# Register loads of TensorE in two separated steps, and the last tiles' upward products in two halves around the downward ones

## What is computed

```python
x = x + tanh(g_xattn) * xattn(layernorm(x), ctx, itok, Wq, Wkv, Wo)   # 16 heads, each query looks at 4 neighbouring keys
h = layernorm(x)
gate_probs = softmax(h @ gate_w.T)          # 8 experts
top_v, top_i = top_k(gate_probs, 2)         # each token goes to two of them
for e in range(8):
    y = silu(h @ w1[e] + b1[e]) @ w2[e] + b2[e]     # 256 -> 1024 -> 256
    out += y * comb_w[..., e]
x = x + tanh(g_ffn) * out
```

## Time and profile before

| | us |
|---|---|
| median of 3 runs | 349.89 |
| lowest and highest | 349.18 and 349.98 |
| the profiled execution | 349.19 |
| its span in the profile | 347.5 |
| TensorE busy | 316.7 |
| VectorE busy | 259.5 |
| POOL busy | 198.0 |
| ScalarE busy | 174.2 |

### The profile page before, as it was taken

The page is one execution under the profiler, slowest core; times in us unless marked ns, Lnnn a source line. Parts: engine busy times, 40 slices in busy tenths (PEclk is TensorE's granted clock), DMA queues, the critical chain, the costliest instruction groups (busy, mean ns, idle before and its releaser), DMA issues.

```text
span 347.5 us, 11173 instructions
## 1 busy us (share of the span) xinstructions
PE 316.7 (91%) x3342; PEld 258.0 (74%) x3342; DVE 259.5 (75%) x593; ACT 174.2 (50%) x490; POOL 198.0 (57%) x227
## 2 busy tenths in 40 slices
PE   7798899999998879999999999999999998999930
PEld 7467788888887767788787887878878786778710
DVE  5769999999998867878788787887878865556620
ACT  2452356565466357656566565665656633253400
POOL 3486889986773142555474655656566463662330
PEclk9999999999999989999999999999999999999985
DMA  7799999998999534354534444445453534353210
GB/s 249 226 375 412 403 420 404 411 408 348 335 380 377 177 80 64 64 63 79 92 59 85 65 79 82 64 90 64 80 78 64 93 52 78 62 84 55 34 21 12
DMA packets 51004, 57.93 MB, mean 167 GB/s; under 512 B 24434, under 2 KB 45154, under 8 KB 48900
## 3 DMA queue, kind: packets, MB, share of 16 engines
q0 software_dynamic: 9408, 26.63, 30.1%
q1 hardware_dynamic: 36212, 27.18, 25.9%
q10 hardware_dynamic: 5328, 3.37, 3.1%
HBM read 42.29 MB, written 10.17 MB: 151 GB/s over the span
## 4 chain that ended last, share of the span: by engine, by line
PE 55%; DVE 23%; DMA 10%; issue 5%; POOL 2%; ACT 2%; POOLq 0%; ACTq 0%; DVEq 0%
PE ps L1151 25%; PE ps L1165 13%; PE ps L1168 7%; DMA out<-sel 6%; DVE ps L1330 5%; DVE sel L1326 3%; DVE w_parts L1326 2%; PE ps L1173 2%; DMA sel<-near_rows,win_near 2%; DVE xs L1362 1%; DVE sel L1601 1%; DVE xn L1598 1%; PE ps L987 1%; DVE ps L1334 1%; DMA near_rows<-w_parts 1%
## 5 line engine op out<-in xcount | busy, mean ns | idle before, releaser
L1151 PEld LDWEIGHTS ps<-sel,w_parts 128*128 x1776 | 121.4, 99 | 34.0 <-issue 6.2
L1151 PE MATMUL ps<-sel,w_parts 128*128 128x128 f16 x1776 | 142.4, 221 | 2.7 <-DVE sel L1601 1.1
L879 ACT ACTIVATE sel<-ps,b1T 128x128 f32<-128x128 f32 x296 | 84.6, 370 | 85.8 <-PE ps L1151 84.0
L644 POOL DMA_INDIRECT out<-sel x37 | 64.7, 1748 | 87.2 <-DVE sel L1601 74.5
L1165 PE MATMUL ps<-w_parts,sel 128*128 x259 | 96.4, 380 | 0.4 <-DVE sel L1567 0.2
L1168 PE MATMUL ps<-w_parts,sel 128*128 x259 | 70.6, 273 | 0.0
L1565 DVE TENSOR_SCALAR sel<-sel 128x512 f16<-128x512 f32 x74 | 32.2, 435 | 28.2 <-ACT sel L879 27.5
L1567 DVE SCALAR_TENSOR_TENSOR sel<-sel 128x512 f16<-128x512 f32 x74 | 51.3, 693 | 2.5
L636 POOL DMA_INDIRECT sel<-tokens_split,sel x37 | 40.4, 1092 | 16.2 <-DVE sel L1535 9.3
L1553 DVE SCALAR_TENSOR_TENSOR w_parts<-w_parts (+1 forms) x32 | 39.0, 1225 | 12.9 <-ACT w_parts L858 11.0
L858 ACT ACTIVATE w_parts<-w_parts (+1 forms) x32 | 34.0, 1067 | 7.0 <-issue 4.4
(11 more groups left out here) (229 smaller groups left out, 422.3 us busy)
## 6 DMA issues: line engine op xcount, KB each, us to landing
w_parts<-in_L_ffn_w SPq DMA_DIRECT2D x16, 1024.0 KB
out<-xs SPq DMA_DIRECT2D x16, 128.0 KB
tokens_split<-xsplit ACTq DMA_DIRECT2D x13, 128.0 KB, 5.7
xs<-in_x ACTq DMA_DIRECT2D x2, 512.0 KB, 7.4
xs<-in_x SPq DMA_DIRECT2D x2, 512.0 KB, 7.3
near_rows<-w_parts SPq DMA_DIRECT2D x4, 256.0 KB, 9.5
sel<-tokens_split,sel POOLq DMA_INDIRECT x37, 3.1
out<-sel POOLq DMA_INDIRECT x37
```

The costliest lines, as they stand in the source:

```text
L644: pool.indirect_dma_start(out_rows, bass.IndirectOffsetOnAxis(slot_row[:, at(q - 1)], 0), y_sb[(k + 3) % 4], None, compute_op=ALU.add).the ...
L879: act.activation(h32[n][:, c * P:c * P + P], ps_h[n][:, c * P:c * P + P], ACT.Silu, bias=biases[:, c:c + 1], scale=1.0 / (X_SCALE * W_SCALE))\
L1151: mm = pe.matmul(ps_h[n][:, c * P:c * P + P], w, xx, start=(i == 0), stop=(i == len(products) - 1))
```

## The change

1. `registers_for` loads one table instead of two. `before_of` is loaded at the end of the steps with k = 2 as before, `expert_of` at the end of those with k = 0 (0, 4, ..., 32). The three registers each for tiles 36 to 38 are loaded after steps 5 and 7, not both after step 28. Of the loads ahead of step -1 one of `before_of` is left.
2. From step 31 on the upward block of tile q+1 is cut into chunks 0 to 3 ahead of the downward block of tile q-1 and chunks 4 to 7 behind it, each in its own `filled`. The first half waits also for `silu_ok` of tile q-1, and the downward block waits for the first half of `hlo_ok` at chunk 0 and the second at chunk 4.
3. VectorE splits the first half of tile q+1 ahead of `rows_out` of tile q-1 in the last tiles too.

```diff
-            def registers_for(t):
+            def registers_for(t, registers, table):
                 n, some = register(t), slice(t, min(t + 4, NT))
                 count = some.stop - some.start
-                pe.reg_load(before_of[n:n + count], tile_p[0:1, some])
-                pe.reg_load(expert_of[n:n + count], tile_e[0:1, some])
+                pe.reg_load(registers[n:n + count], table[0:1, some])
...
                 if q == -2:
-                    registers_for(0)
+                    registers_for(0, before_of, tile_p)
...
                 if q + 1 >= FULL:
+                    def up_half(h):
+                        with filled(pe, tiles, q + 1):
+                            first = block_byte(up, E)
+                            if h == 0:
+                                turned(pe, q + 1)
+                                pe.wait_ge(s["silu_ok"], (q - 1) * FC + 4)
+                            for c in range(4 * h, 4 * h + 4):
+                                up_chunk(q + 1, n, c, first)
+
+                    if live(1):
+                        up_half(0)
                     with filled(pe, tiles, q - 1):
                         first = block_byte(down, E - 1)
-                        pe.wait_ge(s["hlo_ok"], q * 2)
                         wait(pe, "y_ok", q - 2)
                         for c in range(FC):
+                            if c % 4 == 0:
+                                pe.wait_ge(s["hlo_ok"], q * 2 - 1 + c // 4)
                             down_chunk(q - 1, n, c, first, down)
                     if live(1):
-                        with filled(pe, tiles, q + 1):
-                            first = block_byte(up, E)
-                            turned(pe, q + 1)
-                            for c in range(FC):
-                                up_chunk(q + 1, n, c, first)
+                        up_half(1)
...
-                if k == 2 and q + 2 < FULL + 4:
-                    if q == 2:
-                        pe.wait_ge(s["rt"], RT_PLACES)
-                    registers_for(q + 2)
-                if q == FULL - 4:
-                    registers_for(FULL + 4)
+                if q == 2:
+                    pe.wait_ge(s["rt"], RT_PLACES)
+                if k == 2 and 0 < q < FULL:
+                    registers_for(q + 2, before_of, tile_p)
+                if k == 0 and q < FULL + 4:
+                    registers_for(q, expert_of, tile_e)
+                if q == 5:
+                    registers_for(FULL + 4, before_of, tile_p)
+                if q == 7:
+                    registers_for(FULL + 4, expert_of, tile_e)
...
-                if q + 1 >= FULL:
-                    if live(-1):
-                        rows_out(q, k, m)
                 if live(1):
                     with filled(dve, tiles, q + 1):
                         halves(q + 1, m, 0)
-                if q + 1 < FULL and live(-1):
+                if live(-1):
                     rows_out(q, k, m)
```

## The result

| | before, us | after, us |
|---|---|---|
| median | 349.89 (7 runs) | 351.86 (7 runs) |
| lowest and highest | 349.13 and 350.21 | 351.13 and 353.26 |
| the profiled execution | 349.19 | 351.86 |
| its span | 347.5 | 350.1 |
| TensorE busy | 316.7 | 319.0 |

The change makes the kernel slower: the ratio is 1.0067, with a 95% interval of 1.0046 to 1.0088. The medians stand 1.97 us apart and the spans 2.6 us. The forecast was 352.6 us, in a range of 350.2 to 354.0.

The account below looks back on a forecast made before the run. The prediction took PE's sequencer to bound the kernel. Its terms, 0.40 + 1.60 + 0.42 + 0.31 = 2.73 us, on the median of 349.89 us gave 352.6 us, with an 8-in-10 range of 350.2 to 354.0.

Parts of the forecast that it names:

- The bound: Whole expert stage: PE's sequencer, not the array, sets the time; four tiles take 21.9 us on both.
- Rival 1: Steady-stretch boundaries: a single load hides under the sequencer's lead, a pair does not; 347.6 us, chance 0.11.
- The moved loads, 0: Steady-stretch boundaries: pairs split into single loads cost 0, since no load disappears and two waits make one.
- The loads of three registers, 0: Pair after step 28, moved to steps 5 and 7: length belongs to the instruction, so cost 0.
- The 0.86 us of the low end: Three-register loads: gain of 2 x 0.43 us if their long duration were chance, counted in the range's low end.
- The new load, +0.40: End of step 0: the `expert_of` load, formerly before step -1, stands on the path with its whole +0.40 us.
- The five heads, +1.60: Steps 31 to 35: one block more each, a branch, a MOVE and a wait, about 0.32 us a step.
- the end, +0.42 and +0.31: Step 35 and last scatters: down(34) starts later behind the first upward half, +0.42 us; the scatter chain adds +0.31.
- VectorE's order, 0: Last tiles: halves ahead of `rows_out` cost nothing, filling time in which down(q-1) still runs.
- Rival 3: Last tiles: a tile's transpose lands too late for the earlier first upward half; 354.6 us, chance 0.03.

Follow-up runs that it names:

- e10b: The changed kernel with VectorE's old order in the last tiles (`rows_out` ahead of the halves again): 351.31 us, ratio 1.0047.
- e5: The kernel before with six redundant four-register loads of `before_of` more, midway between the pairs: 350.67 us, ratio 1.0032.
- e8: The kernel before with eight-register loads in pairs after steps 6, 14, 22 and 30, in rings of sixteen: 348.49 us, ratio 0.9963.
- e9: The kernel before with the whole upward block ahead of the downward one in the last tiles, VectorE's order as in the change: 352.59 us, ratio 1.0069.
- e4: The kernel before with the pair of loads after step 28 reading four registers from tile 35 on instead of three: 350.29 us, ratio 1.0020.
- e7: The kernel before with the pair after step 28 reading four registers from tile 36 on, tables one column wider: 348.95 us, ratio 0.9970.
- e3b: The changed kernel with the `expert_of` load after step 0 back at the head of step -1: 350.66 us, ratio 1.0035.
- e2: The kernel before with only the change's upward halves and VectorE order in the last tiles, loads still in pairs: 351.81 us, ratio 1.0060.
- e6: The kernel before with the last tiles' upward block cut into two filled blocks, both behind the downward block: 350.57 us, ratio 1.0027.

## Why the prediction was right, and where not

1. **The bound.** It was TensorE's sequencer, as told. The column "rest" shows it best: fourteen traces with 7 to 22 loads of 5.3 to 8.7 us have 5.24 to 5.28 us a tile once the time in loads is taken off, against the 5.27 us that the forecast read out of three tiles. Rival 1, a single load that hides under the lead, has fallen: it needed 5.4 us a tile over the 29 tiles of the steady stretch, 156.6 us, and the changed kernel took 160.5. A second sign wasn't looked for. In the profiled execution of the changed kernel TensorE's granted clock was 0.50, the lower of its two levels (1.2 GHz), from 125.9 to 129.4 us; in e10b's it was 1.00. The array spent 4.70 us on tile 0's upward block for e10b's 3.87, and step 1 still began 8.57 us behind the block's first weight load (124.78 to 133.35), in e10b 8.64 (124.99 to 133.63). The kernel before had the same 0.50 from 125.1 to 128.5 us, and its 8.66 us to the first downward weight load are those of e5, e8 and e9 at 1.00. A slower array lost nothing, as it must be where the sequencer sets the pace.
2. **The moved loads, 0.** The step that was mis-sized. It took the loads' durations as theirs wherever they stand. Apart from each other they were shorter, by 0.8 us together on average (0.28 us in the two profiled executions, no more than two executions of the same program differ). The sign of the whole didn't hang on it.
3. **The loads of three registers, 0.** Right: 0.775 and 0.782 us at their new places. The guess that the length belongs to the instruction is borne out by e4 and e7: how many registers a load reads and where it begins in the table set its length. The Trainium skill, page "Runtime: NRT & Kernel Launch", section "Instruction fetch mechanics", has about 200 ns a register. By it four would be longer than three; the trace has 0.33 us for four and 0.77 for three, so it agrees only for registers that are fetched one by one, at 0.26 us each here. The 0.86 us of the low end were not chance, but were to be had by another way, as e7 shows.
4. **The new load, +0.40.** The wait ahead of step 1 grew by 0.48 us and shrank again in e3b; over the stretch from tile 0's upward block it is 0.3 to 0.5 us where the tokens are in time. Right in place and size; in the time it wasn't resolved, and where the tokens are late little of it is left.
5. **The five heads, +1.60, and the end, +0.42 and +0.31.** Together 2.33; measured from step 30 to the last scatter 2.24 in the changed kernel, 2.09 in e2. A tile takes 5.93 us (5.9 forecast). The three scatters were forecast for 330.54, 334.81 and 339.08 us and stand at 330.65, 334.70 and 338.90. The size is right, but its working in part by luck. The head of 0.33 us in the rows above is the first half's, and before, the upward block had all of it but the wait; what a step has more is the branch, the FUSED_REGOPS in an address computation's place and the wait's EVENT_SEMAPHORE, by their distances in the changed kernel 0.137 + 0.021 + 0.106 = 0.26 us. e6 has 0.12 to 0.14 for the first two, where the forecast had 0.21, and e9 0.04 for the wait. So 0.07 to 0.15 of the 0.33 us a tile aren't any of the three instructions. They come with the order of the halves, and what causes them is open.
6. **VectorE's order, 0.** Right, by e10b's scatters. Rival 3, a transpose that is late, didn't come: no wait of the last downward and upward blocks is put down to a DMA.

The balance: 0.48 + 2.24 - 0.8 = 1.9 us, and the medians stand 1.97 us apart. The forecast had 2.73, too much by the shorter loads. The first two terms are from two executions and the third is an average over nine; with the two executions' own 0.28 it is 2.4 us, and their spans are 2.6 apart.

## What to carry to other kernels

When an engine is 91% busy, put its sequencer's row beside the array's for the same line, and compare the two over several tiles: if the lead returns to nothing, the sequencer's instructions are the time, and moving them about changed nothing here but their own length. Then make them fewer or shorter. Here a table that is read from a multiple of four registers on, eight at a time and one table at a time, gave 2.7 us, more than any order of the work did. In a short tail with a chain of transfers at its end, look first at when the first link starts: a block moved ahead of it is paid in full.

## What the hardware showed that was not expected

- A register load from on-chip memory took 0.33 us for four registers that begin at a multiple of four in the table, 0.59 for eight and 1.11 for sixteen, but 0.77 for three and 1.01 to 1.06 for four that begin at 35.
- A load or a pair was 0.2 us longer on average when the last one was 22 us ago than when it was 11 us ago (50 against 74 cases, without those after step 2, which don't follow the pattern). The cause is open.
- The sequencer's lead over the array stops growing: at 1.19 to 1.24 us in the interleaved steps (e8).
- A COMPARE_BRANCH more and a FUSED_REGOPS in place of an ALU_OP cost 0.12 to 0.14 us a step in e6; with an additional wait and the halves apart it was 0.33 us.
- TensorE's granted clock was 0.50 for 3.4 us while the sequencer set the pace, and no time was lost by it (8.57 us against 8.64 at 1.00).
